# Moving the coarse part of a causal mask into free rows of the score contraction, in a differential attention + feed-forward kernel on one Trainium2 core

## The reference

```
q = (x @ Wq) * 4**-0.5 ; k = x @ Wk      # 32 maps, d = 4
v = x @ Wv                               # 16 heads, 8 wide
scores = where(causal, q k^T, -inf) ; probs = softmax(scores)
attn = (probs[map 0] - lam * probs[map 1]) @ v     # lam from lq1, lk1, lq2, lk2
attn = attn * rsqrt(mean(attn^2) + 1e-5) * rms_w * (1 - LAMBDA_INIT)
x = layernorm(x + attn @ Wo)
x = layernorm(x + sigmoid(xr @ Wr^T) * (relu(xk @ Wk^T)^2 @ Wv^T))   # xr, xk mix x with its previous token
```

## Time and profile before

| what | value |
|---|---|
| median of 3 runs | 507.19 us |
| the profiled execution | 505.25 us |
| its span, first to last instruction | 503.5 us |
| busy: PE, DVE, ACT, POOL | 418.9, 391.2, 354.7, 198.2 us |
| mean granted TensorE clock | 0.891 |

### The profile page before, as it was taken

The page is one execution under the profiler, slowest core; times in us unless marked ns, Lnnn a source line. Parts: engine busy times, 40 slices in busy tenths (PEclk is TensorE's granted clock), DMA queues, the critical chain, the costliest instruction groups (busy, mean ns, idle before and its releaser), DMA issues.

```text
span 503.5 us, 14453 instructions
## 1 busy us (share of the span) xinstructions
PE 418.9 (83%) x5191; PEld 178.7 (35%) x5191; DVE 391.2 (78%) x504; ACT 354.7 (70%) x687; POOL 198.2 (39%) x349
## 2 busy tenths in 40 slices
PE   5665788898989898989898989889898978788682
PEld 3431323233434333333333333334242423344352
DVE  2769889797979999979797979898979894324633
ACT  3620168687878888968797969897969687756343
POOL 7000021253535364535354535545444445351512
PEclk9875569798979999979898979999989899989978
DMA  7695202011111120202020202020202010000001
GB/s 204 187 296 227 86 0 69 20 44 44 48 40 44 44 85 0 85 0 85 0 85 0 85 0 85 0 85 0 85 0 85 0 44 4 1 1 22 2 21 42
DMA packets 21082, 28.35 MB, mean 56 GB/s; under 512 B 3776, under 2 KB 8768, under 8 KB 21056
## 3 DMA queue, kind: packets, MB, share of 16 engines
q1 hardware_dynamic: 20624, 27.80, 17.5%
q10 hardware_dynamic: 432, 0.20, 0.2%
HBM read 18.29 MB, written 9.44 MB: 55 GB/s over the span
## 4 chain that ended last, share of the span: by engine, by line
PE 68%; ACT 15%; DVE 8%; issue 6%; DMA 1%; POOL 1%; ACTq 0%; POOLq 0%; DVEq 0%
PE acc L593 28%; PE ex L562 17%; ACT e_buf L898 11%; PE mx L516 7%; PE mx L508 6%; DVE part_max L989 5%; PE mx L690 1%; PE ex L624 1%; ACT o_tok L828 1%; PE ex L629 1%; PE mx L691 1%; DMA x_tok<-in_L_attn_x 1%; PE mx L675 1%; PE mx L710 1%; DVE rest L949 1%
## 5 line engine op out<-in xcount | busy, mean ns | idle before, releaser
L989 DVE TENSOR_REDUCE part_max<-mx 128x2 f32<-128x1024 f32 (+2 forms) x288 | 337.6, 1219 | 45.9 <-PE mx L508 35.8
L898 ACT ACTIVATE e_buf<-ex 128x512 f32<-128x512 f32 x576 | 312.1, 597 | 85.4 <-PE ex L562 81.0
L593 PE MATMUL acc<-e_buf,v_grp 128*32 128x256 f32 (+2 forms) x2200 | 185.5, 424 | 0.0
L562 PE MATMUL ex<-qe,ke 32*128 32x512 bf16 (+3 forms) x768 | 119.0, 346 | 44.0 <-ACT e_buf L898 29.2
L435 POOL TENSOR_SCALAR_AFFINE_SELECT e_buf<-e_buf 128x512 f32<-128x512 f32 x128 | 78.9, 634 | 169.5 <-ACT e_buf L898 169.4
L508 PE MATMUL mx<-km,qm 32*128 32x128 bf16 (+2 forms) x1280 | 124.4, 284 | 13.6 <-DVE part_max L989 12.1
L562 PEld LDWEIGHTS ex<-qe,ke 32*128 32x128 bf16 x768 | 30.9, 92 | 168.1 <-ACT e_buf L898 159.1
L593 PEld LDWEIGHTS acc<-e_buf,v_grp 128*32 128x32 f32 x2200 | 50.1, 115 | 65.6 <-issue 56.1
L508 PEld LDWEIGHTS mx<-km,qm 32*128 32x128 bf16 x1280 | 43.6, 96 | 25.9 <-DVE part_max L989 22.1
L516 PE MATMUL mx<-mask,pick 32*128 32x384 bf16 (+3 forms) x512 | 47.4, 308 | 0.0
L419 POOL TENSOR_TENSOR r_rms<-sq_eps,minus_half 128x16 f32<-128x16 f32 x15 | 43.7, 2910 | 1.2
(11 more groups left out here) (130 smaller groups left out, 266.3 us busy)
## 6 DMA issues: line engine op xcount, KB each, us to landing
qm<-q_rows SPq DMA_DIRECT2D x16, 256.0 KB, 2.7
km<-k_rows SPq DMA_DIRECT2D x16, 256.0 KB, 2.9
qe<-q_rows SPq DMA_DIRECT2D x16, 256.0 KB, 2.9
ke<-k_rows SPq DMA_DIRECT2D x16, 256.0 KB, 3.0
x_tok<-in_L_attn_x SPq DMA_DIRECT2D x2, 512.0 KB, 5.0
q_rows<-zero_rows SPq DMA_DIRECT2D x2, 512.0 KB, 5.8
k_rows<-ones_rows SPq DMA_DIRECT2D x2, 512.0 KB, 7.5
out<-v_all SPq DMA_DIRECT2D x4, 256.0 KB, 2.3
```

Of the source, the lines that this page charges most:

```text
L562: scored = pe.matmul(ex[:, ex_slot(b, i) % EX_BANKS, col:col + w], ke[par][rows, P * kb:P * (kb + 1)], qe[par][rows, q1 - w:q1], start=col ...
L593: last = pe.matmul(bank[STRIP * j:STRIP * (j + 1), hi - w:hi], v_grp[par][:, kb, j // 2, shift:shift + STRIP], e_buf[:, k % ESLOTS, j, col ...
L898: nc.scalar.activation(e_buf[:, k % ESLOTS, 2 * p + i, :], ex[:, ex_slot(b, i) % EX_BANKS, :], ACT.Exp).then_inc(s["exped"], 1)
L989: nc.vector.tensor_reduce(target, mx[m % 2][:].rearrange("p s (a b) -> p s a b", a=a), AX.X, ALU.max).then_inc(s["maxed"], 1)
```

## The change

Inter-chunk masking moves into the contraction. The layout of a strip becomes 6 terms x 4 dims (`"s (g d) t"`), so that the 24 term rows come first and the 8 fillers last. Fillers 0 and 1 are those of the maxima. Fillers 2 to 4 are new: in q row 2+i is 1 for tokens of chunk i of their 128-block (chunks of 32 tokens), in k it is -1e30 for tokens of later chunks. In masked units the contraction takes 29 rows (`ROWS`), elsewhere and in the exp pass 26 (`COARSE`), where it took 32. The mask matmuls keep only the 32 x 32 triangles: four pairs of 128 columns. POOL makes the fillers from two 8 x 4 tiles: two memsets, three affine selects and four copies into 8-partition tiles, in place of two 128 x 1024 memsets. `write_parts` issues one transfer for each term: 12 a call, where it was 6.

```
-FILL = len(TERMS)
+FILL = len(TERMS) * D
+COARSE = FILL + 2
+ROWS = COARSE + 3
...
+    q_parts = q_rows.rearrange("s (g d) t -> s d g t", d=D)
+    q_fill = q_rows.rearrange("s r t -> r s t")[FILL:STRIP]
...
-            def fill_rows(rows, done):
-                for target, fill in ((q_parts, zero_rows), (k_parts, ones_rows)):
-                    sp.dma_start(target[rows, FILL:ROW_GROUP, :],
-                                 fill[:].unsqueeze(1).broadcast_to([P, ROW_GROUP - FILL, S])).then_inc(done, 16)
+            def fill_rows(b, done):
+                subs = slice(NSUB // B * b, NSUB // B * (b + 1))
+                for target, fill in ((q_fill, q_fills), (k_fill, k_fills)):
+                    sp.dma_start(target[:, subs, :],
+                                 fill[:].rearrange("r b c t -> r (b c t)").unsqueeze(1)
+                                 .broadcast_to([STRIP - FILL, NSUB // B, S])).then_inc(done, 16)
...
-                        sp.dma_start(target[rows, at[0]:at[-1] + 1:step, :],
-                                     parts[w][part][own, b, :].unsqueeze(1)
-                                     .broadcast_to([own.stop - own.start, len(at), S])).then_inc(done, 16)
+                        for i in (i for i, term in enumerate(TERMS) if term[w] == part):
+                            sp.dma_start(target[subs, :, i, :], parts[w][part][own, b, :]).then_inc(done, 16)
...
-            sp.wait_ge(s["ones_set"], 2)
+            sp.wait_ge(s["fills_set"], 9)
...
-            pool.memset(ones_rows[:], -1.0).then_inc(s["ones_set"], 1)
-            pool.memset(zero_rows[:], 0.0).then_inc(s["ones_set"], 1)
+            pool.memset(q_chunks[:], 0.0).then_inc(s["fills_set"], 1)
+            pool.memset(k_chunks[:], NEG).then_inc(s["fills_set"], 1)
+            fill_steps = [
+                (q_chunks, ALU.not_equal, 1.0, 2, -1, 1),
+                (k_chunks, ALU.is_ge, 0.0, 1, -1, 1),
+                (k_chunks, ALU.is_ge, -1.0, -2, 1, 0),
+            ]
+            for i, (t, op, fill, base, by_row, by_chunk) in enumerate(fill_steps):
+                pool.wait_ge(s["fills_set"], i + 2)
+                pool.affine_select(out=t[:], in_=t[:], compare_op=op, fill=fill, base=base,
+                                   pattern=[[by_chunk, SUBS]], channel_multiplier=by_row).then_inc(s["fills_set"], 1)
+            for i, (t, chunks) in enumerate(((q_fills, q_chunks), (k_fills, k_chunks))):
+                for h in range(2):
+                    pool.wait_ge(s["fills_set"], 5 + 2 * i + h)
+                    pool.tensor_copy(t[:, NB // 2 * h:NB // 2 * (h + 1)],
+                                     chunks[:].unsqueeze(1).unsqueeze(3)
+                                     .broadcast_to([STRIP - FILL, NB // 2, SUBS, STRIP])).then_inc(s["fills_set"], 1)
...
             def max_unit(n, par, m):
+                used = ROWS if masked else COARSE
...
-                        rows = slice(STRIP * j, STRIP * (j + 1))
+                        rows = slice(STRIP * j, STRIP * j + used)
...
-                        cols = mask[rows, c, STRIP * c:P].unsqueeze(1).broadcast_to([STRIP, 4, P - STRIP * c])
-                        last = pe.matmul(mx[m % 2][:, jj, :].rearrange("p (a t) -> p a t", a=4)[:, :, STRIP * c:P],
+                        own = slice(STRIP * c, STRIP * (c + 1))
+                        cols = mask[rows, c, own].unsqueeze(1).broadcast_to([STRIP, 4, STRIP])
+                        last = pe.matmul(mx[m % 2][:, jj, :].rearrange("p (a t) -> p a t", a=4)[:, :, own],
                                          pick[rows, c, :], cols, start=False, stop=c == SUBS - 1,
...
             def score_pair(n, par, b):
-                        rows = slice(STRIP * j, STRIP * (j + 1))
+                        rows = slice(STRIP * j, STRIP * j + COARSE)
```

More of the change, by code:

```diff
@@ L28 @@
 TERMS = [(0, 1), (0, 2), (0, 0), (1, 0), (2, 0), (1, 1)]
-ROW_GROUP = STRIP // D
-FILL = len(TERMS)
+FILL = len(TERMS) * D
+COARSE = FILL + 2
+ROWS = COARSE + 3
 MAX_UNITS = [
@@ L116, in build @@
     k_group = k_rows.rearrange("(n j) r t -> n (j r) t", j=SUBS)
-    q_parts = q_rows.rearrange("s (d g) t -> (s d) g t", g=ROW_GROUP)
-    k_parts = k_rows.rearrange("s (d g) t -> (s d) g t", g=ROW_GROUP)
+    q_parts = q_rows.rearrange("s (g d) t -> s d g t", d=D)
+    k_parts = k_rows.rearrange("s (g d) t -> s d g t", d=D)
+    q_fill = q_rows.rearrange("s r t -> r s t")[FILL:STRIP]
+    k_fill = k_rows.rearrange("s r t -> r s t")[FILL:STRIP]
     HEAD = 2 * SUBS * D
@@ L150, in build @@
         identb = sb("identb", [P, P], BF16)
-        ones_rows = sb("ones_rows", [P, S], BF16)
-        zero_rows = sb("zero_rows", [P, S], BF16)
+        q_chunks = sb("q_chunks", [STRIP - FILL, SUBS], BF16)
+        k_chunks = sb("k_chunks", [STRIP - FILL, SUBS], BF16)
+        q_fills = sb("q_fills", [STRIP - FILL, NB, SUBS, STRIP], BF16)
+        k_fills = sb("k_fills", [STRIP - FILL, NB, SUBS, STRIP], BF16)
         mask_zero = sb("mask_zero", [P, SUBS, P], BF16)
@@ L210, in build @@
         names = """x_in0 x_in1 wqk_in wv_in w_in small_in bounce_in rms_in
-                   ident ones_set mask_set vpad_set xcol_set
+                   ident fills_set mask_set vpad_set xcol_set
                    xt_done xt_copied_a xt_copied_d proj_done hi_done rest_done mid_done lo_done
@@ L280, in _ @@
                 sp.dma_start(wf_sb[:, i, :], w).then_inc(s["w_in"], 16)
-            def fill_rows(rows, done):
-                for target, fill in ((q_parts, zero_rows), (k_parts, ones_rows)):
-                    sp.dma_start(target[rows, FILL:ROW_GROUP, :],
-                                 fill[:].unsqueeze(1).broadcast_to([P, ROW_GROUP - FILL, S])).then_inc(done, 16)
+            def fill_rows(b, done):
[4 more added lines that the diff above has]
+                                 .broadcast_to([STRIP - FILL, NSUB // B, S])).then_inc(done, 16)
             def write_parts(b, own, done):
-                rows = slice(b * P + own.start, b * P + own.stop)
+                subs = slice((b * P + own.start) // D, (b * P + own.stop) // D)
                 for part, need in ((0, "hi_done"), (1, "mid_done"), (2, "lo_done")):
@@ L292, in write_parts @@
                     for w, target in enumerate((q_parts, k_parts)):
-                        at = [i for i, term in enumerate(TERMS) if term[w] == part]
-                        step = at[1] - at[0] if len(at) > 1 else 1
-                        sp.dma_start(target[rows, at[0]:at[-1] + 1:step, :],
-                                     parts[w][part][own, b, :].unsqueeze(1)
-                                     .broadcast_to([own.stop - own.start, len(at), S])).then_inc(done, 16)
-            sp.wait_ge(s["ones_set"], 2)
-            fill_rows(slice(0, P), s["rows_head"])
+                        for i in (i for i, term in enumerate(TERMS) if term[w] == part):
+                            sp.dma_start(target[subs, :, i, :], parts[w][part][own, b, :]).then_inc(done, 16)
+            sp.wait_ge(s["fills_set"], 9)
+            fill_rows(0, s["rows_head"])
             for i, m in enumerate((mu_r, mu_k)):
@@ L307, in _ @@
             write_parts(0, slice(0, HEAD), s["rows_head"])
-            sp.wait_ge(s["rows_head"], 16 * (2 + 6))
+            sp.wait_ge(s["rows_head"], 16 * (2 + 2 * len(TERMS)))
             load_max_rows(sp, 0, 0)
@@ L312, in _ @@
             load_exp_rows(sp, 0, 0)
-            fill_rows(slice(P, 2 * P), s["rows_b1"])
+            fill_rows(1, s["rows_b1"])
             write_parts(1, slice(0, P), s["rows_b1"])
@@ L324, in group @@
                     place_maxima(sp, n + 1, 1 - par, visit + par)
-            sp.wait_ge(s["rows_b0"], 16 * 6)
+            sp.wait_ge(s["rows_b0"], 16 * 2 * len(TERMS))
             group(0, 0, 0)
             group(1, 1, 0)
-            sp.wait_ge(s["rows_b1"], 16 * (2 + 6))
+            sp.wait_ge(s["rows_b1"], 16 * (2 + 2 * len(TERMS)))
             with sp.Fori(1, NG // 2 - 1) as i:
```

## The result

The kernel after takes 519.56 us (median of 4, 518.59 to 523.0) against 507.12: ratio 1.0254, 95% interval 1.0213 to 1.0295. It is 2.5% slower, where 491 and 481 to 501 were forecast. The profiled execution took 519.63 us, its span is 517.9.

A forecast was written before the change was run, and what follows sets the result against it. ACT and DVE were taken to bound b 14 to b 5, PE b 6 to b 13. Groups -15.7, first masked units -2.1, start +1.7 gave -16.1 us: 489.1 profiled, 491 in the runs, range 481 to 501.

The forecast's parts named there:

- the sum stays as it is while the cover above holds: Start transfers: group 0's load goes out at 23.0, still 4 us of cover, so slower filler transfers add nothing.
- not late: Start: the load of first maxima and exp operands lies beside DVE's eight units of group 1, so costs nothing.
- double at most: Start transfers: an outermost dimension under 16 limits the engines, so fillers' and batch 0 parts' shares double at most.
- The mask matmuls: Masked steps: narrow masks take 0.23 us, not 0.54, saving 0.31 a unit, 1.24 a group at full clock.
- What reaches the group: Full-clock groups: PE allows 1.24 us, DVE's slacks 1.19, so each group becomes 1.19 shorter, about 21.9 us.
- under 0.2 was forecast: Sign in DVE's timeline: its wait at b 6, 0.77 us before, falls under 0.2 in full-clock groups.
- The clock: Low-clock stretches behind light steps b 4 and 5: their average cost, 1.43 us a group, stays as it is.
- The rival: Another low-clock stretch behind the masked steps in every group, 2.4 us each, giving 525 us; chance 0.07.
- The masked units ahead of the first exp: Eight masked units before the first exp step: shorter masks remove most of DVE's 2.3 us wait, saving 2.1.
- POOL: Start: POOL's new filler work takes 4.9 us in place of 1.9, its identities ready at 7.0, not 3.99.
- the term that was 1.7: Start: PE's first transposes come 1.8 us late behind POOL, of which 1.7 is carried to the first maximum unit.
- 26 rows for 32: Score and maximum matmuls: contracting 26 or 29 rows of 32 costs nothing, as two maps' matmuls still overlap.

The follow-up runs named there:

- e5: The kernel after with fillers read from 128-partition tiles in four transfers a batch, filler rows outermost in DRAM, mask between chunks left out: 496.4 us.
- e7: The kernel after with fillers spread by way of DRAM and repeated maximum matmuls: ten in unit 12, two each in units 11 and 13: 477.62 us.
- e8: The kernel after with fillers by way of DRAM and extra 128-row matmuls of 512 columns, three in unit 12, one in unit 13: 483.02 us.
- e9: The kernel before with only e7's repeated matmuls added (ten in unit 12, two each in units 11 and 13): 487.21 us.
- e3: The kernel after with the fillers written once to an 8-row DRAM tensor and spread from there to all strips: 496.2 us.
- e1: The kernel before with mask matmuls narrowed to their own 32 columns per block, mask between chunks left out of the maximum pass: 493.69 us.
- e10: The kernel after with fillers by way of DRAM and repeated matmuls, six, ten and four in units 11, 12 and 13: 492.26 us.
- e4: The kernel after with fillers by way of DRAM and repeated maximum matmuls, six in unit 12, two in unit 13: 489.68 us.

## Why the prediction was wrong

**The step that failed: "the sum stays as it is while the cover above holds", of the transfers at the start.** It priced the fillers by bytes and at most by half the engines, with 4 us of cover. They moved at 52 GB/s, where 128 partitions gave 179 in the same order of the destination. And they did not only land late: SP issues in order, and behind them four small issues took 18 us together, so that everything after these went out late too. The load of group 0 went out at 37.14, not 23.0, and PE waited 12.9. The prediction looked at what is queued behind the fillers for batch 0 only. For batch 1 the same two transfers held back the placing of the first maxima, which it called "not late": 11.3 us. That it is the 8-partition source is shown by the kernel after and e5, which write the fillers in the same order. They differ in the number of transfers (two and four a batch) and in POOL's work as well, but the time of a packet, 293 ns for 84, is the source's. Why such a source is slow was not tried.

The page "DMA: Bandwidth & Descriptors" of the Trainium skill (Rules for kernel authors), cited there, holds as to engines: the share of 0.53 with the filler rows outermost is half of 1.05. It was not the bound. The prediction took "double at most" from it as if nothing else could slow a transfer. No row had 8 partitions as a source, so its rate was unknown, and a slow one belonged among the rivals.

**The mask matmuls: right.** 0.33 was to stand from the start of the masks to that of the sums; the timeline of PE of the kernel after, b 10, has 0.32 (218.01 to 218.33):

```profile
217.68 0.39 PE L583 MATMUL ex<-qe,ke 26*128 26x512 bf16 x2
...
218.01 0.39 PE L537 MATMUL mx<-mask,pick 32*128 32x128 bf16 x8
218.33 0.64 PE L614 MATMUL acc<-e_buf,v_grp 128*32 128x256 f32 x8
218.91 0.39 PE L583 MATMUL ex<-qe,ke 26*128 26x512 bf16 x2
```

**What reaches the group: 0.91, not 1.19.** A full-clock group is 22.22 (211.31 to 233.53), for 23.13. The starts of the steps b 12, b 13 and b 14 of the kernel after show where:

```profile
197.91 0.39 PE L583 MATMUL ex<-qe,ke 26*128 26x512 bf16 x2
...
199.06 0.39 PE L583 MATMUL ex<-qe,ke 26*128 26x512 bf16 x2
...
200.62 0.39 PE L583 MATMUL ex<-qe,ke 26*128 26x512 bf16 x2
```

The step from b 12 to b 13 is 1.15, for 1.45 before. The one from b 13 to b 14 is 1.56, for 1.61 before, so three masked steps gave 0.2 to 0.3 each and the fourth next to nothing. The prediction let the step at b 13 pass like the others, but it also turns the maxima. At b 6 DVE still waits 0.54 (under 0.2 was forecast), so DVE was not the limit. ACT has no gap from the exps of b 11 until it has copied the turned maxima, and PE's scores of b 14 start at 200.62, in that copy:

```profile
197.20 3.37 ACT L919 ACTIVATE e_buf<-ex 128x512 f32<-128x512 f32 x6 [0.24 <-PE ex L583]
200.45 0.25 ACT L856 COPY max_rows<-ex 64x128 bf16<-64x128 bf16 x1
```

These rows point to ACT's exps and the three banks as what sets that step; it wasn't tried by itself. DVE's wait at b 6:

```profile
213.30 1.23 DVE L1010 TENSOR_REDUCE part_max<-mx 128x4 f32<-128x1024 f32 x1 [0.54 <-PE mx L528]
```

**The clock: left as it was, and it took some back.** Twelve groups average 24.00, so the low clock costs 1.78 a group, not 1.43. The rival had it come behind the masked steps; it came where it was, behind b 4 and 5, and took 0.35 a group of the 0.91. With the masks alone it was less (23.84 over the same twelve). The page "TensorE: Matmul & The Clock Gate" of the Trainium skill (A second HAM failure mode: psum-queue depth-cycling) reports that PE's idling between groups of matmuls does this. The traces agree, for work put into the steps around b 4 and 5 takes most of it away: of twelve groups eight have a fall in the kernel before, nine in the kernel after, four in e7, one in e8 and none in e9. How many groups have a fall, and how long, differs between kernels with the same step costs, and what sets that stays open.

**The masked units ahead of the first exp: right within a us; POOL: priced too high.** With masks alone the first turned sums are 3.5 us earlier; 2.1 and group 0's 0.7 were forecast. POOL's fillers put PE's first transposes from 5.18 to 5.89, not to 7.0: the four copies of 8x512 took 0.65 each, waits included, not 0.84. PE's first maximum unit, in e3 and in e1:

```profile
28.88 0.40 PE L532 MATMUL mx<-km,qm 29*128 29x128 bf16 x8 [1.37 <-DVE turn_max L1037]
```

```profile
27.86 0.40 PE L508 MATMUL mx<-km,qm 32*128 32x128 bf16 x8 [1.37 <-DVE turn_max L1013]
```

In the kernel before it starts at 28.85, though its code up to there is e1's. So two traces of one start differ by 1.0 us: 1.0 of e1's 3.5 us is not the masks', and the term that was 1.7 measured between 0.0 and 1.0 (0.3 at the first turned sums, 89.95 in e3 for 89.69 in e1). **26 rows for 32: nothing, right**: 512 score columns take 0.39 in pairs, as in the kernel before.

Put together, with the start mended the change is worth 496.2 against 508.2, 12 us, for the 16 of the prediction's sum. In the two profiled executions it is 9.5: 3.3 up to the first turned sums, 7.2 in twelve groups, where 14.3 was forecast, and 1.0 lost behind them. Of the 7.1 missing in the groups 3.4 are the 0.28 a group that the steps gave less, and the rest is mostly the clock.

## What to carry to other kernels

Where a change gives a transfer a new shape, its rate is unknown until a row has that shape: here a source of 8 partitions, read 32 times, gave 52 GB/s where 128 partitions gave 179. Price what stands behind it in the issuing queue as well, for each time that it is issued. And where a group has steps in which PE idles and the clock falls behind them, harmless PE work in these steps can be worth more than the work that a change removes elsewhere: here 20.9 us against 12. Too much of it costs: e10 took 492.26 us, e7 477.62.

## What the runs showed of the hardware

Each busy DMA engine moved about 7 GB/s (52 GB/s at a share of 0.46) out of a source of 8 SBUF partitions that was read 32 times over, 21 to 24 GB/s out of 128 partitions. Behind two such transfers of 512 KB an issue on the same queue took 3.5 to 5 us, for 0.5 to 1.1 in the kernel before. In the 2 us up to half a us past the start of the turned sums PE had 1.01 or 1.02 us of work in the kernel before (0.94 in the first group), and the granted clock went to 0.50 behind eight of twelve such places; with 1.67 (e4, 1.59 in the first group) it fell behind ten, and with 2.00 behind none (e9), one (e8), two (e10) or four (e7).
